# Node degrees by one-hot products: a count matrix of 64 rows by 98 columns in place of 128 by 49

## The chip, the cores and the metric

The kernel runs on one NeuronCore of a Trainium2 chip. The metric is the device time of one execution in microseconds (us). Three runs of the kernel before gave 1557.44 us as their median (1555.77 to 1563.06).

## The reference, cut to what matters

The program is one layer of a graph network over N = 6250 nodes with 256 features and E = 100,000 edges: layer norm, a graph convolution, a linear attention, and a mixture of experts. The change touches one term of the graph convolution, the number of edges that end in each node:

```python
deg = jax.ops.segment_sum(jnp.ones_like(dst_f, dtype=h.dtype), dst_f, num_segments=n)
dinv = jax.lax.rsqrt(deg)
norm = dinv[src_f] * dinv[dst_f]
out = jax.ops.segment_sum(h[src_f] * norm[:, None], dst_f, num_segments=n) + conv_bias
```

`dst_f` holds the 100,000 edge targets and one self loop per node, so deg is the count of edges into a node, plus one.

## The kernel before, in words

The kernel is a sequence of phases with a barrier of all engines between them. The change lies in the first one, which prepares the statistics, the degrees and the table of scaled node rows. Nodes lie as 49 tiles (T) of 128 partitions (P): node n is partition n mod 128 of tile n div 128.

**Preparation.** The edge targets are loaded as 98 rows of 512 (L239), turned by TensorE transposes of 98 by 128 blocks (L428), and copied out by ScalarE (L281) as 784 columns (NC) of 128 edges. VectorE splits each target into hi = target >> 7 and lo = target & 127 (L509, L510) and stores both as bf16 (L511, L512).

**Counting.** The 784 columns are taken in 56 blocks (OHB) of 14 (OHC). For each block VectorE writes two one-hot tiles by comparing with an iota: `ohlo`, 128 values by 14 columns (L533), and `ohhi`, 49 values by 14 columns (L534). TensorE then issues 14 products per block (L447), one per column c: stationary `ohlo[:, :, c]` (128 columns) and moving `ohhi[:, :, c]` (49 columns), both bf16, all summed into one PSUM tile of 128 by 49, which is the degree of node (partition, tile). The block's column is the last dimension of the one-hot tiles, so that neighbouring elements of both operands of a product lie 14 elements (28 bytes) apart. A ring of four pairs of tiles (OHR) joins the two engines: VectorE waits on `oh_free` (L530) before it overwrites a pair, TensorE on `oh_ok` (L445) before it reads one. Two products with an all-zero tile open and close the sum (L442, L450). There are 56 x 14 = 784 counting products.

**Beside it.** ScalarE computes sums (L290) and squared sums (L295) of the node rows. GpSimd (POOL) builds constants (L346 to L370), then waits for these sums and turns them into layer norm statistics (L375 to L395). VectorE's program has two reciprocals for them between its blocks: L541 stands after block 48, behind a wait for GpSimd, and L546 after block 52, behind a wait for ScalarE's square root (L310).

**After the count.** VectorE waits for the closing product, adds one (L553), ScalarE takes the square root (L312), VectorE forms the inverse root and the scale and bias of every node row (L556 to L563). Only then ScalarE scales the 49 tiles (L321), TensorE turns them (L456), VectorE and GpSimd copy them, and SP writes them to the table in memory (L265). The next phase gathers from that table.

A second stage later in the kernel has the same form and isn't touched: L1506 counts expert places by 14 products per round with a stationary of 128 columns and a moving operand of 105 columns, both bf16 and both 28 bytes apart from element to element.

Of the kernel before, what the change touches and what calls it, by code (L numbers as in the profile page):

```python
# [4 lines left out]
f32, i32, bf16, f16 = mybir.dt.float32, mybir.dt.int32, mybir.dt.bfloat16, mybir.dt.float16  # L5
i16 = mybir.dt.int16
ALU, ACT, AX = mybir.AluOpType, mybir.ActivationFunctionType, mybir.AxisListType
P = 128
# [6 lines left out]
T = -(-N // P)  # L15
# [8 lines left out]
OHC = 14  # L24
# [30 lines left out]
def build(nc, a_x, a_src, a_dst, a_gw, a_cb, a_lnw, a_lnb, a_pre, a_wqkv, a_mk, a_mv, a_wout, a_bout,  # L55
# [5 lines left out]
    with ExitStack() as ctx:  # L61
        def sb(name, shape, dt=f32):
            return ctx.enter_context(nc.sbuf_tensor(name, shape, dt))

        def semaphore(phase, name):

            phase.append(nc.alloc_semaphore(name))
            return phase[-1]
# [7 lines left out]
        R2 = sb("R2", [P, KC * NP])  # L76
# [36 lines left out]
        ident = sb("ident", [P, P])  # L113
# [18 lines left out]
        deg = sb("deg", [P, T])  # L132
# [20 lines left out]
        ps = [ctx.enter_context(nc.psum_tensor(f"ps{i}", [P, 512], f32)) for i in range(8)]  # L153
# [4 lines left out]
        class Chain:  # L158
# [5 lines left out]
            def done(self, ins):  # L164
# [12 lines left out]
        dTi = R3[:, 7000:7000 + NC].bitcast(i32)  # L177
        hiI = R3[:, 7800:7800 + NC].bitcast(i32)
        loI = R3[:, 8600:8600 + NC].bitcast(i32)
        hiB = R3[:, 9400:9400 + NC // 2].bitcast(bf16)  # L180
        loB = R3[:, 9800:9800 + NC // 2].bitcast(bf16)
        iox = RG[:, 0:P * OHC // 2].bitcast(bf16).rearrange("p (j c) -> p j c", c=OHC)
        ohlo = [R2[:, 1250 * k:1250 * k + P * OHC // 2].bitcast(bf16).rearrange("p (j c) -> p j c", c=OHC)
                for k in range(OHR)]
        ohhi = [R2[:, 1250 * k + 900:1250 * k + 900 + T * OHC // 2].bitcast(bf16).rearrange("p (j c) -> p j c", c=OHC)
                for k in range(OHR)]
        slowT = R3[:, 10200:10200 + NC].rearrange("p (g c) -> p g c", c=GC)
        zeroB = slotb[:, 0, 0:P // 2].bitcast(bf16)
        zslot = RG[:, 0:ZS * D].rearrange("p (s f) -> p s f", s=ZS)
        root3, val3, tmp3 = (RG[:, 3560 + 3 * T * k:3560 + 3 * T * (k + 1)] for k in range(3))  # L190
# [11 lines left out]
        phase = []  # L202
        with nc.Block() as block:
# [17 lines left out]
            oh_ok = semaphore(phase, "p_onehots_ready")  # L221
            oh_free = semaphore(phase, "p_onehots_free")
            deg_ok = semaphore(phase, "p_deg_ready")
            slow_ok = semaphore(phase, "p_outside_ready")
            slow_out = semaphore(phase, "p_outside_stored")
            root_in = semaphore(phase, "p_root_in")
# [110 lines left out]
            def _(pool):  # L337
                n = 0

                def step(ins):  # L340
# [7 lines left out]
                                             base=0, pattern=[[-1, P]], channel_multiplier=1))  # L348
# [9 lines left out]
                                             base=0, pattern=[[1, P]], channel_multiplier=-1))  # L358
                step(nc.gpsimd.affine_select(out=valid[:, :], in_=ones[:, 0:1], compare_op=ALU.is_gt, fill=0.0,
                                             base=TAIL, pattern=[[0, 1]], channel_multiplier=-1))  # L360
                step(nc.gpsimd.memset(inblk, 0.0))
                for a, b in DBLK:
                    step(nc.gpsimd.tensor_copy(inblk[:, a:b], ident[:, a:a + 1].to_broadcast([P, b - a])))
                step(nc.gpsimd.affine_select(out=isd[:, 0:1], in_=ones[:, 0:1], compare_op=ALU.is_gt, fill=0.0,
                                             base=ND, pattern=[[0, 1]], channel_multiplier=-1))
                step(nc.gpsimd.affine_select(out=isd[:, 1:2], in_=ones[:, 0:1], compare_op=ALU.is_ge, fill=float(WIN // DW),
                                             base=-ND, pattern=[[0, 1]], channel_multiplier=1))
# [2 lines left out]
                step(nc.gpsimd.tensor_copy(iokey[:, :], iokey_i))  # L370
                pool.sem_inc(const, 1)

                var, two = sc[:, :], slice(0, 2 * T)
                pool.wait_ge(sum_ok, 2 * T + 1)
                step(nc.gpsimd.tensor_scalar(var, ssq[:, :], 1.0 / D, None, ALU.mult))  # L375
# [38 lines left out]
            @block.tensor  # L414
            def _(pe):
                pe.sem_inc(oh_free, OHR)
                pe.sem_inc(zt_ok, 4)
                pe.wait_ge(const, 1)
                for n, arr in enumerate((dstf, relf, srcf)):
                    if n == 1:  # L420
                        pe.wait_ge(const, 3)
                        pe.wait_ge(least_ok, 1)
                        nc.tensor.matmul(ps[6][0:GH, 500:501], inblk[0:GH, 0:GH], least[0:GH, 0:1], start=True,
                                         stop=True).then_inc(first_ok, 1)
                    pe.wait_ge(rel_ok, n + 1)
                    for h in range(2):
                        for c in range(GC):
                            last = nc.tensor.transpose(ps[2 * n + h][:, c * GH:(c + 1) * GH],  # L428
                                                       arr[0:GH, h, c * P:(c + 1) * P], ident[0:GH, 0:GH])
                        last.then_inc(tr_ok, 1)  # L430

                pe.wait_ge(rel_ok, 4)
                for k in range(4):
                    nc.tensor.transpose(ps[6][0:1, k * GH:(k + 1) * GH], cols[0:GH, k:k + 1], ident[0:GH, 0:GH])
                pe.wait_ge(tr_ev, 1)
                for k in range(GC + 1):
                    last = nc.tensor.transpose(ps[0][0:1, k * GH:(k + 1) * GH], cols[0:GH, 4 + k:5 + k],
                                               ident[0:GH, 0:GH])
                last.then_inc(bt_ok, 1)

                pe.wait_ge(oh_ok, 1)
                nc.tensor.matmul(ps[7][:, 0:T], zeroB, zeroB[:, 0:T], start=True, stop=False)  # L442
                with nc.tensor.Fori(0, OHB // OHR) as i:
                    for k in range(OHR):
                        pe.wait_ge(oh_ok, i * OHR + (k + 2))  # L445
                        for c in range(OHC):
                            last = nc.tensor.matmul(ps[7][:, 0:T], ohlo[k][:, :, c], ohhi[k][:, :, c],  # L447
                                                    start=False, stop=False)
                        last.then_inc(oh_free, 1)
                nc.tensor.matmul(ps[7][:, 0:T], zeroB, zeroB[:, 0:T], start=False, stop=True).then_inc(deg_ok, 1)  # L450

                def flip(t, u):
                    pe.wait_ge(z_ok, t + 1)
                    pe.wait_ge(zt_ok, t + 1)
                    for k in range(KC):
                        last = nc.tensor.transpose(ps[u % 4][:, k * P:(k + 1) * P], zslot[:, u, k * P:(k + 1) * P],  # L456
                                                   ident[:, :])
                    last.then_inc(zt_ps, 1)

                with nc.tensor.Fori(0, T // ZS) as i:  # L460
                    for u in range(ZS):
                        flip(i * ZS + u, u)
                flip(T - 1, 0)

            @block.vector
            def _(v):
# [3 lines left out]
                ch = Chain(v, dv)  # L470
                v.wait_ge(d_in, 16 * 2)
                h = slice(0, GH)
# [18 lines left out]
                for c in range(GC):  # L491
                    last = nc.vector.tensor_scalar(relf[h, 0, c * P:(c + 1) * P], dstf[h, 0, c * P:(c + 1) * P],
                                                   cut[h, c:c + 1], None, ALU.subtract)
# [12 lines left out]
                v.wait_ge(tr_ev, 2)  # L506
                dflat = dT.rearrange("p g c -> p (g c)")
                ch.done(nc.vector.tensor_copy(dTi, dflat))
                ch.done(nc.vector.tensor_scalar(hiI, dTi, 7, None, ALU.arith_shift_right))  # L509
                ch.done(nc.vector.tensor_scalar(loI, dTi, P - 1, None, ALU.bitwise_and))  # L510
                ch.done(nc.vector.tensor_copy(hiB, hiI))  # L511
                ch.done(nc.vector.tensor_copy(loB, loI))  # L512

# [15 lines left out]
                def onehots(m, k):  # L529
                    v.wait_ge(oh_free, m + 1)  # L530
                    lo = loB[:, bass.ds(m * OHC, OHC)].unsqueeze(1)
                    hi = hiB[:, bass.ds(m * OHC, OHC)].unsqueeze(1)
                    nc.vector.tensor_tensor(ohlo[k], lo.to_broadcast([P, P, OHC]), iox, ALU.is_equal)  # L533
                    nc.vector.tensor_tensor(ohhi[k], hi.to_broadcast([P, T, OHC]), iox[:, 0:T, :],  # L534
                                            ALU.is_equal).then_inc(oh_ok, 1)

                with nc.vector.Fori(0, OHB // OHR - 2) as i:
                    for k in range(OHR):
                        onehots(i * OHR + k, k)
# [3 lines left out]
                for k in range(OHR):  # L543
                    onehots(OHB - 2 * OHR + k, k)
# [3 lines left out]
                for k in range(OHR):  # L548
                    onehots(OHB - OHR + k, k)

                v.wait_ge(deg_ok, 1)
                inv, fix = root3[:, 2 * T:3 * T], tmp3[:, 2 * T:3 * T]
                ch.done(nc.vector.tensor_scalar(deg[:, :], ps[7][:, 0:T], 1.0, None, ALU.add))  # L553
                v.sem_inc(root_in, 1)
                v.wait_ge(root_ok, 2)
                ch.done(nc.vector.reciprocal(inv, inv))  # L556
# [88 lines left out]
        phase = []  # L645
# [536 lines left out]
        phase = []  # L1182
# [146 lines left out]
        phase = []  # L1329
# [490 lines left out]
        phase = expert_phase  # L1820
# [222 lines left out]
```

## Time and profile before

| what | value |
|---|---|
| median of 3 runs | 1557.44 us (1555.77 to 1563.06) |
| the profiled execution | 1565.51 us |
| its span | 1563.7 us |
| TensorE matmuls (PE) busy | 1295.5 us, 83% |
| TensorE weight loads (PEld) busy | 1132.9 us, 72% |
| VectorE (DVE) busy | 987.5 us, 63% |
| GpSimd (POOL) busy | 870.6 us, 56% |
| ScalarE (ACT) busy | 525.8 us, 34% |

The busy shares are means over phases with different limits. For this change the first 145 us matter: the preparation up to about 26 us, the counting from about 26 to 111 us, and the scaled rows and the table from about 112 to 141 us. A matmul's duration in the rows is its latency, which overlaps with that of the next; how fast a series goes is read from the distance between starts.

### The profile page before, as it was taken

What the parts mean: (1) busy time and instruction counts of PE and PEld (TensorE: products, weight loads), DVE (VectorE), ACT (ScalarE), POOL (GpSimd) and SP (SyncE); (2) the same over time, 40 slices, a digit from 0 to 9 for tenths busy, and PEclk for the clock granted to TensorE, in tenths of its full rate; (3) what the DMA queues carried; (4) which work ended last, traced back from release to release, by engine and by line L of the source; (5) the groups of instructions that cost most, each with busy time, mean ns of one, the idle gap of its engine ahead of it and who ended that gap; (6) DMA issues with size and microseconds to landing.
All of it is one profiled execution on the core that took longest, in us unless ns stands there. A gap on an engine that the chain in (4) does not pass through costs nothing. (4 is left out here: it accounts for less than half of the span.)

```text
span 1563.7 us, 30532 instructions
## 1 busy us (share of the span) xinstructions
PE 1295.5 (83%) x8310; PEld 1132.9 (72%) x8311; DVE 987.5 (63%) x2911; ACT 525.8 (34%) x1415; POOL 870.6 (56%) x837
## 2 busy tenths in 40 slices
PE   4986587878867788879878879788569999999996
PEld 4974476767757677768767667566359999999996
DVE  7987466656556777667677548777844444444443
ACT  6608000111112222323331120133735555555553
POOL 2374666666666666666666631133027766676664
PEclk9998787999989999999998988899569999999998
DMA  7006332332345555556677760032944444444442
GB/s 216 0 0 208 88 88 86 88 89 85 88 125 146 151 166 169 172 170 190 193 237 225 244 199 1 14 108 95 331 53 71 68 69 70 66 74 69 72 66 35
DMA packets 138352, 183.07 MB, mean 117 GB/s; under 512 B 27256, under 2 KB 116036, under 8 KB 138124
## 3 DMA queue, kind: packets, MB, share of 16 engines
q0 software_dynamic: 44400, 92.92, 25.7%
q1 hardware_dynamic: 93852, 89.00, 19.0%
q8 instruction: 41, 0.67, 0.2%
q14 instruction: 59, 0.48, 0.1%
HBM read 149.38 MB, written 33.41 MB: 117 GB/s over the span
## 5 line engine op out<-in xcount | busy, mean ns | idle before, releaser
L729 POOL DMA_INDIRECT RG<-table,srci x504 | 492.1, 976 | 283.8 <-issue 126.9
L746 PEld LDWEIGHTS ps<-S_t,RG 128*128 128x128 f32 x2016 | 283.2, 208 | 32.7 <-issue 17.0
L746 PE MATMUL ps<-S_t,RG 128*128 128x96 f32 x2016 | 284.8, 288 | 16.7 <-issue 12.6
L1000 DVE TENSOR_TENSOR R<-R,ps 128x392 f32 x280 | 157.5, 562 | 184.2 <-PE ps L756 77.9
L768 PE MATMUL ps<-zrow,R 128*128 128x256 f32 x686 | 205.5, 404 | 30.9 <-DMA zrow<-table 16.4
L1990 POOL DMA_INDIRECT out<-R,S_t x105 | 166.7, 1588 | 98.3 <-DVE R L1960 55.0
L1873 PE MATMUL ps<-R,RG 128*128 128x128 f32 x1680 | 206.8, 277 | 0.0
L1883 PE MATMUL ps<-R 128*128 x840 | 198.5, 379 | 0.0
L1873 PEld LDWEIGHTS ps<-R,RG 128*128 128x128 f32 x1680 | 197.8, 193 | 0.3 <-issue 0.3
L1906 ACT ACTIVATE R<-ps,RG 128x128 f32<-128x128 f32 x420 | 120.1, 368 | 175.2 <-PE ps L1873 139.1
L1956 DVE TENSOR_TENSOR R<-ps,R 128x256 f32<-128x256 f32 x105 | 44.6, 425 | 200.6 <-PE ps L1883 198.8
L768 PEld LDWEIGHTS ps<-zrow,R 128*128 128x128 f32 x686 | 127.5, 200 | 56.6 <-DMA zrow<-table 27.2
L1883 PEld LDWEIGHTS ps<-R 128*128 128x128 f32 x840 | 151.7, 190 | 16.3
L1978 POOL DMA_INDIRECT R<-ntable,S_t x105 | 104.4, 994 | 90.1 <-PEq L1855 58.4
L872 ACT ACTIVATE R<-iwin 128x256 f32<-128x256 f32 (+2 forms) x127 | 60.3, 488 | 204.5 <-PE ps L768 131.8
L1915 ACT ACTIVATE RG<-R 128x1028 f32 x105 | 112.7, 1075 | 20.5 <-PEq L72 20.5
L1567 POOL TENSOR_TENSOR R<-R,slot 128x256 f32<-128x256 f32 x49 | 35.6, 728 | 111.1 <-DVE slot L1651 111.1
L447 PE MATMUL ps<-R 128*128 128x49 bf16 x784 | 80.7, 276 | 10.1 <-DVE R L534 10.0
L447 PEld LDWEIGHTS ps<-R 128*128 128x128 bf16 x784 | 72.8, 144 | 18.0 <-DVE R L534 11.9
L756 PE MATMUL ps<-ohk,ohs 128*128 128x392 bf16 x140 | 48.8, 350 | 33.4 <-issue 19.6
L1945 DVE TENSOR_SCALAR R<-ps,gamma,beta 128x128 f32<-128x128 f32 x212 | 76.2, 400 | 0.0
L959 DVE TENSOR_TENSOR S_t<-dstrel,iwin 128x384 f32<-128x384 f32 x126 | 69.4, 550 | 0.7
(362 smaller groups left out, 2026.3 us busy)
## 6 DMA issues: line engine op xcount, KB each, us to landing
zrow<-table SPq DMA_DIRECT2D x336, 128.0 KB
RG<-table,srci POOLq DMA_INDIRECT x504
table<-RG SPq DMA_DIRECT2D x12, 512.0 KB, 3.0
out<-R SPq DMA_DIRECT2D x12, 512.0 KB, 2.9
ntable<-R SPq DMA_DIRECT2D x12, 512.0 KB
R<-in_x SPq DMA_DIRECT2D x6, 896.0 KB
R<-in_w SPq DMA_DIRECT2D x8, 514.0 KB, 9.0
slot<-in_x SPq DMA_DIRECT2D x32, 128.0 KB
```

What stands on the lines that cost most here:

```text
L447: last = nc.tensor.matmul(ps[7][:, 0:T], ohlo[k][:, :, c], ohhi[k][:, :, c], start=False, stop=False)
L729: nc.gpsimd.indirect_dma_start(out=grows[:, s, :], out_offset=None, in_=table, in_offset=bass.IndirectOffsetOnAxis(ap=srci[:, ND + q, c:c ...
L746: last = nc.tensor.matmul(window(q % 2)[:, h, :], grows[:, s, h * P:(h + 1) * P], S_t[:, q % 2, c, :], start=c == 0, stop=c == GC - 1)
L768: nc.tensor.matmul(psD[:, 0:D], adj[b % 2][0:n, j, :], zrow[0:n, i % ZR, :], start=j == 0, stop=j == T - 1).then_inc(z_used, 1)
L1000: nc.vector.tensor_tensor(win, win, psK[m % 2][:, 0:T * DW].rearrange("p (j w) -> p j w", w=DW), ALU.add).then_inc(cnt_ok, 1)
L1873: last = nc.tensor.matmul(psH[s % 2][:, h * P:(h + 1) * P], w1r[:, s, k * HID + h * P:k * HID + (h + 1) * P], ur[:, s % 2, k, :], start=k ...
L1883: last = nc.tensor.matmul(psY[s % 2][:, 0:D], hr[:, s % 2, h, :], w2_sb[:, bass.ds(e, 1), h, :].rearrange("p a f -> p (a f)"), start=h == ...
L1906: last = act.activation(hr[:, s % 2, h, :], psH[s % 2][:, h * P:(h + 1) * P], ACT.Gelu, bias=w1r[:, s, KC * HID + h:KC * HID + h + 1])
L1915: act.activation(w1r[:, s, :], w1_sb[:, bass.ds(e, 1), :].rearrange("p a f -> p (a f)"), ACT.Copy).then_inc(c_ok, 1)
L1945: nc.vector.tensor_scalar(ur[:, s % 2, k, :], psX[s % 2][:, k * P:(k + 1) * P], gamma[:, k:k + 1], beta[:, k:k + 1], ALU.mult, ALU.add)
L1978: nc.gpsimd.indirect_dma_start(out=xr[:, t % 4, :], out_offset=None, in_=ntable, in_offset=bass.IndirectOffsetOnAxis(ap=gat[:, t:t + 1], a ...
L1990: nc.gpsimd.indirect_dma_start(out=a_out, out_offset=bass.IndirectOffsetOnAxis(ap=sct[:, t:t + 1], axis=0), in_=yr[:, t % 4, :], in_offset ...
```

## The change

The count matrix is 64 by 98: lo is now the low six bits of the target, hi the rest. The stationary one-hot tile has 64 columns, the moving one 98. At the end the two halves of a tile's 128 nodes lie in neighbouring columns of 64 rows. VectorE copies them apart into SBUF (`halfT`), and two fp32 products put them under each other in another PSUM bank: one with the upper 64 rows of the identity, one with a matrix `upper` that shifts by 64 rows, which GpSimd builds among its constants. The one-hot ring's tiles in SBUF are laid out anew for the new sizes. The number of blocks, their 14 columns, the ring of four, and the number of counting products stay.

```diff
+        cols2 = R2[:, 5100:5100 + 2 * T + P]
+        LO = P // 2
-        ohlo = [R2[:, 1250 * k:1250 * k + P * OHC // 2].bitcast(bf16).rearrange("p (j c) -> p j c", c=OHC)
+        ohlo = [R2[:, 1250 * k:1250 * k + LO * OHC // 2].bitcast(bf16).rearrange("p (j c) -> p j c", c=OHC)
                 for k in range(OHR)]
-        ohhi = [R2[:, 1250 * k + 900:1250 * k + 900 + T * OHC // 2].bitcast(bf16).rearrange("p (j c) -> p j c", c=OHC)
+        ohhi = [R2[:, 1250 * k + 500:1250 * k + 500 + T * OHC].bitcast(bf16).rearrange("p (j c) -> p j c", c=OHC)
                 for k in range(OHR)]
+        halfT, upper = cols2[:, 0:2 * T], cols2[:, 2 * T:2 * T + P]
...
+                step(nc.gpsimd.memset(upper, 0.0))
+                step(nc.gpsimd.affine_select(out=upper, in_=upper, compare_op=ALU.not_equal, fill=1.0, base=LO,
+                                             pattern=[[-1, P]], channel_multiplier=1))
+                pool.sem_inc(half_ok, 1)
...
-                            last = nc.tensor.matmul(ps[7][:, 0:T], ohlo[k][:, :, c], ohhi[k][:, :, c],
+                            last = nc.tensor.matmul(ps[7][0:LO, 0:2 * T], ohlo[k][:, :, c], ohhi[k][:, :, c],
                                                     start=False, stop=False)
...
-                nc.tensor.matmul(ps[7][:, 0:T], zeroB, zeroB[:, 0:T], start=False, stop=True).then_inc(deg_ok, 1)
+                nc.tensor.matmul(ps[7][0:LO, 0:2 * T], zeroB[:, 0:LO], zeroB[:, 0:2 * T], start=False,
+                                 stop=True).then_inc(deg_ok, 1)
+                pe.wait_ge(half_ok, 2)
+                nc.tensor.matmul(ps[6][:, 0:T], ident[0:LO, :], halfT[0:LO, 0:T], start=True, stop=False)
+                nc.tensor.matmul(ps[6][:, 0:T], upper[0:LO, :], halfT[0:LO, T:2 * T], start=False,
+                                 stop=True).then_inc(deg_ok, 1)
...
-                ch.done(nc.vector.tensor_scalar(hiI, dTi, 7, None, ALU.arith_shift_right))
-                ch.done(nc.vector.tensor_scalar(loI, dTi, P - 1, None, ALU.bitwise_and))
+                ch.done(nc.vector.tensor_scalar(hiI, dTi, 6, None, ALU.arith_shift_right))
+                ch.done(nc.vector.tensor_scalar(loI, dTi, LO - 1, None, ALU.bitwise_and))
...
-                    nc.vector.tensor_tensor(ohlo[k], lo.to_broadcast([P, P, OHC]), iox, ALU.is_equal)
-                    nc.vector.tensor_tensor(ohhi[k], hi.to_broadcast([P, T, OHC]), iox[:, 0:T, :],
+                    nc.vector.tensor_tensor(ohlo[k], lo.to_broadcast([P, LO, OHC]), iox[:, 0:LO, :], ALU.is_equal)
+                    nc.vector.tensor_tensor(ohhi[k], hi.to_broadcast([P, 2 * T, OHC]), iox[:, 0:2 * T, :],
                                             ALU.is_equal).then_inc(oh_ok, 1)
...
                 v.wait_ge(deg_ok, 1)
+                ch.done(nc.vector.tensor_copy(halfT[0:LO, :].rearrange("p (h t) -> p h t", h=2),
+                                              ps[7][0:LO, 0:2 * T].rearrange("p (t h) -> p h t", h=2)))
+                v.sem_inc(half_ok, 1)
+                v.wait_ge(deg_ok, 2)
-                ch.done(nc.vector.tensor_scalar(deg[:, :], ps[7][:, 0:T], 1.0, None, ALU.add))
+                ch.done(nc.vector.tensor_scalar(deg[:, :], ps[6][:, 0:T], 1.0, None, ALU.add))
```

## Rows read from the trace of the kernel before

**Rows 1.** Groups by line, 0 to 260 us: count, busy us, mean ns, idle before.

```profile
L447 PE MATMUL ps<-R 128*128 128x49 bf16 x784 | 80.7, 276 | 10.1 <-DVE R L534 10.0
L533 DVE TENSOR_TENSOR R<-R,RG 128x1792 bf16<-128x1792 bf16 x56 | 61.7, 1101 | 0.7 <-DVE flag_i L526 0.3 <-DVE RG L546 0.2 <-DVE RG L541 0.2
```

**Rows 2.** Timeline, first blocks and steady state: start us, us, what.

```profile
26.23 1.09 DVE L533 TENSOR_TENSOR R<-R,RG 128x1792 bf16<-128x1792 bf16 x1 [0.34 <-DVE flag_i L526]
27.24 0.51 DVE L534 TENSOR_TENSOR R<-R,RG 128x686 bf16<-128x686 bf16 x1
27.80 1.31 PEld L447 LDWEIGHTS ps<-R 128*128 128x128 bf16 x14 [7.13 <-DVE R L534]
...
43.38 1.08 DVE L533 TENSOR_TENSOR R<-R,RG 128x1792 bf16<-128x1792 bf16 x1
44.38 0.51 DVE L534 TENSOR_TENSOR R<-R,RG 128x686 bf16<-128x686 bf16 x1
44.81 1.08 DVE L533 TENSOR_TENSOR R<-R,RG 128x1792 bf16<-128x1792 bf16 x1
```

**Rows 3.** Timeline, one late block by itself, and the end of the count.

```profile
101.13 1.51 PE L447 MATMUL ps<-R 128*128 128x49 bf16 x14 [0.22 <-DVE R L534]
...
111.51 0.22 PE L450 MATMUL ps<-slotb 128*128 128x49 bf16 x1
111.77 0.21 DVE L553 TENSOR_SCALAR deg<-ps 128x49 f32<-128x49 f32 x1 [1.65 <-PE ps L450]
...
114.36 6.01 ACT L321 ACTIVATE RG<-R,zs_b,zs_s 128x256 f32<-128x256 f32 x12 [2.04 <-DVEq L564]
```

**Rows 4.** Timeline of the second counting stage, its first two rounds.

```profile
1121.89 5.61 PE L1506 MATMUL ps<-R 128*128 128x105 bf16 x28 [7.55 <-DVE R L1772]
```

**Rows 5.** Lines L1506 and L1502: duration ns min/median/max, first and last start.

```profile
L1506 PE MATMUL ps<-R x98: 368/373/391, 1121.9 to 1142.4; 128*128 128x105 bf16 x98
...
L1502 PE MATMUL ps<-slotb x1: 271/271/271, 1114.1 to 1114.1; 128*128 128x105 bf16 x1
```

**Rows 6.** Two stretches: length, PE busy us, granted clock, DMA share, GB/s.

```profile
28.00:95.00 67.00, 67.00 (x659) 1.00 0.01 2
...
1122.00:1142.00 20.00, 18.90 (x96) 0.50 1.22 261
```

**Rows 7.** Timeline: fp32 transposes, and weight loads in pairs.

```profile
7.07 1.54 PE L428 MATMUL ps<-ident,R 98*128 98x98 f32 x8 [7.07 <-DVEq L475]
...
120.42 0.29 PEld L456 LDWEIGHTS ps<-ident,RG 128*128 128x128 f32 x2 [0.20 <-ACT RG L321]
120.91 0.20 PEld L456 LDWEIGHTS ps<-ident,RG 128*128 128x128 f32 x2 [0.20 <-ACT RG L321]
```

**Rows 8.** Timeline of L1492: loads of 49 columns for products of one column.

```profile
1108.33 1.57 PEld L1492 LDWEIGHTS ps<-ones,R 128*49 128x49 f32 x16 [10.08 <-DVEq L1717]
```

**Rows 9.** Timeline: an fp32 product, its reader, and a PSUM read of 98 columns.

```profile
11.34 0.49 PE L423 MATMUL ps<-least,S_t 98*98 98x1 f32 x2 [2.73 <-POOLq L368]
...
11.94 0.16 DVE L482 COPY cols<-ps 98x1 f32<-98x1 f32 x1 [2.35 <-PE ps L423]
...
25.08 0.25 DVE L524 CAST first_i<-ps 1x98 int32<-1x98 f32 x1
```

**Rows 10.** Timeline of GpSimd's constants and statistics, and of what they release.

```profile
0.79 0.20 POOL L346 MEMSET ident<- 128x128 f32 x1 [0.29 <-POOLq L2033]
1.24 0.29 POOL L347 TENSOR_SCALAR_AFFINE_SELECT ident<-ident 128x128 f32<-128x128 f32 x1 [0.25 <-POOL ident L346]
...
63.28 31.82 POOL L375 TENSOR_SCALAR sc<-ssq 128x49 f32<-128x49 f32 x1 [50.84 <-ACT slot L295]
...
95.62 0.47 DVE L541 RECIPROCAL RG<-RG 128x49 f32<-128x49 f32 x1 [0.74 <-POOLq L377]
...
97.81 0.29 ACT L310 ACTIVATE RG<-RG 128x98 f32<-128x98 f32 x1 [33.32 <-POOLq L381]
...
109.95 0.38 POOL L395 TENSOR_SCALAR cq<-cq 128x49 f32<-128x49 f32 x1
```

More of the change, by code:

```diff
@@ L223, in build @@
             deg_ok = semaphore(phase, "p_deg_ready")
+            half_ok = semaphore(phase, "p_half_rows")
             slow_ok = semaphore(phase, "p_outside_ready")
@@ L441, in _ @@
                 pe.wait_ge(oh_ok, 1)
-                nc.tensor.matmul(ps[7][:, 0:T], zeroB, zeroB[:, 0:T], start=True, stop=False)
+                nc.tensor.matmul(ps[7][0:LO, 0:2 * T], zeroB[:, 0:LO], zeroB[:, 0:2 * T], start=True, stop=False)
                 with nc.tensor.Fori(0, OHB // OHR) as i:
```

## The prediction

> **What bounds the kernel now.** I read the groups by line for the stage first: 784 counting products and 56 pairs of one-hot writes, and nearly all idle time that TensorE has before a counting product (10.0 of 10.1 us) ends with VectorE's second one-hot write, L534 [rows 1]. Then the timeline, to see who sets the pace. VectorE starts L533 at 43.38, L534 at 44.38 and the next L533 at 44.81: 1.00 us for 1792 elements and 0.43 us for 686, so 1.43 us a block and no gap [rows 2]. TensorE's own pace shows where a block stands alone: 14 products in 1.51 us of which the last 0.276 us are its latency, so 13 distances in 1.234 us, 95 ns each [rows 1, 3], 1.33 us a block. VectorE bounds the count, by 1.43 to 1.33: TensorE has 7% to spare. The count is wholly on the path. After its closing product at 111.51 come L553 on VectorE at 111.77, and the scaled rows on ScalarE only from 114.36 [rows 3]; a barrier ends the phase, so what the count gains or loses moves the rest of the kernel.
>
> **The change on VectorE.** From the two sizes, (1.00 - 0.43) us / (1792 - 686) = 0.515 ns an element and about 0.08 us fixed [rows 2]. The new tiles have 64 x 14 = 896 and 98 x 14 = 1372 elements: 0.54 and 0.78 us, 1.32 us a block. That is 0.11 us less, 6.2 us over 56 blocks, if VectorE stayed the bound.
>
> **The change on TensorE.** The products stay 784, and each moves 98 columns in place of 49. What a moving column costs in this layout, 28 bytes from one to the next, is the number on which all hangs, and there are two rows for it. At 49 columns the distance is 95 ns [rows 1, 3]. The second counting stage has the same stationary tile of 128 columns, the same 28 bytes, and 105 moving columns: 28 products in 5.61 us, less the last one's 0.373 us, is 27 distances of 194 ns [rows 4, 5]. So 56 columns more cost 99 ns, 1.77 ns each, and 98 columns give 95 + 49 x 1.77 = 182 ns. A plain ratio, 194 x 98 / 105, gives 181. That the distance between columns in memory is the cause shows in the latency: with the closely packed zero tile a product of 105 columns took 271 ns, the spaced ones 373 [rows 5]; at 49 columns it is 0.22 us against 276 ns [rows 1, 3].
>
> Both rows must stand for the same clock to be set on one line. The second stage has 0.50, the lower level of 1.2 GHz. The profile shows 1.00 for the first [rows 6], but I don't believe it: L428's eight transposes of 98 columns, of which the last has 0.37 us of latency, start 0.167 us apart, and the loads of L456 fall from 0.29 to 0.20 us a pair only between 120.42 and 120.91 [rows 7]. The packed products agree: 0.22 us at 49 columns [rows 3] and 271 ns at 105 [rows 5] differ by 0.86 to 0.9 ns a column, one cycle of 1.2 GHz. So the count ran at the lower level from start to end, and the rise came behind it.
>
> Here the Trainium skill speaks on both sides. "SBUF — State Buffer" says of reads that each access which leaves a 16-byte line pays a penalty; at 28 bytes each moving column does, and the trace agrees (373 against 271 ns). "TensorE: Matmul & The Clock Gate", section "Back-to-back issue gap", gives N/1.2 ns at the lower clock, 82 ns for 98 columns, with which TensorE would stay under VectorE; by the same rule 105 columns take 88 ns, where the trace has 194, so the rows decide.
>
> TensorE then needs 14 x 182 = 2.55 us a block against VectorE's 1.32: the bound changes sides. Rows for the price run from 1.67 ns a column (0.167 us for L428's 98 fp32 columns [rows 7]: 164 ns) to 1.94 (95 ns for 49 [rows 3]: 190 ns). I take 182, which lies between two rows of this very form.
>
> **Weight loads.** 64 stationary columns in place of 128. No row has this load in bf16. The nearest narrow one is L1492: 16 loads of 49 columns in 1.57 us, about 93 ns each with its product of one column [rows 8]; scaled to 64 columns 122 ns. From below it is nothing. In the second stage loads of 128 columns lie beside products of 194 ns without making them longer than the line above, so I put 122 under 182 at nothing. If that cover failed, it would be a rival, below.
>
> **Sum for the count.** The first pair of tiles is ready at 26.23 + 0.54 + 0.86 (the second's full duration, 0.78 + 0.08) = 27.63, the first load 0.05 us later, as 27.80 follows 27.24 + 0.51 now [rows 2]: 27.68. From there TensorE runs without a gap, since the ring of four fills: 784 x 0.182 = 142.7, hence the closing product at 170.3 in place of 111.51: +58.8. At the 181.5 between both estimates, which I use, it is +58.5. VectorE now waits on oh_free (L530) over a microsecond in each block.
>
> **What stands behind that wait.** The reciprocal L541 follows block 48, which VectorE can write once block 44 is consumed: 27.7 + 44 x 2.54 = 139 us. GpSimd's L375 took 31.82 us, until VectorE paused, and L541 came at 95.62, so GpSimd seems kept out by VectorE's writes [rows 10]; pauses in each block let it in sooner. From L541 to ScalarE's root at 97.81 is 2.2 us, from there to the last statistics at 109.95 is 12 us, and TensorE has four blocks (10 us) and then four more in hand. Both hide, also with 2 us more. Without that cover each would cost its 2.2 us.
>
> **Tail.** Added on the path between L450 and L553: the copy of 98 columns from PSUM, 0.25 us, and two fp32 products. One product, from its start to its reader, is 11.94 - 11.34 = 0.60 us, and a second adds up to its 0.49 [rows 9]. With two hand-overs of about 0.05 us: 1.4 us. Ends: 0.9 and 2.0.
>
> **The rest.** GpSimd's memset and select, 0.20 and 0.29 us, with their own waits under 1 us [rows 10], lie at about 12.4 us; GpSimd idles 50.84 us until 63.28 [rows 10], and `half_ok` is wanted only at 170. Shift and mask keep their sizes. No DMA is added.
>
> Sum: +58.5 + 1.4 = **+59.9 us**. The profiled execution's 1565.5 would become 1625.4; it stands 8.1 us over the median. On the median: 1557.4 + 59.9 = **1617.3 us**.
>
> **Rivals.**
> 1. *The loads don't hide.* A narrow load that can't go in beside the running product adds its 122 ns: 784 x 0.304 = 238 us, +154.5 in place of +58.5, 1713 us. For it: no row has such a load beside a long product, and the Trainium skill ("TensorE: Matmul & The Clock Gate", section "Weight-path perf modes") keeps its fast load for 128 columns. Against: at 128 columns loads and products overlap [rows 4].
> 2. *The clock rises in the count, and TensorE keeps up (not slower).* If it goes to 2.4 GHz in the middle of the work and the spaced reads halve with it, the distance is 91 ns, 1.27 us a block, under VectorE's 1.32. Then VectorE saves 6.2 us, the tail costs 1.4: 1552.6 us. It decides from 94 ns (1.32 us / 14) down. For it: the fp32 loads did fall with the clock [rows 7]. Against: the second stage, busy 18.90 of 20.00 us with products of nearly this form, stayed at 0.50 [rows 6].
> 3. *Spacing costs latency, not pace.* Then what holds the products apart is something else that doesn't grow with the columns, and 98 of them stay near 95 ns, 1.33 us a block: level with VectorE's 1.32, some 1553 us. It decides from the same 94 ns. Against it are the 194 ns at 105 columns [rows 4]. This is the mechanism that the Trainium skill's gap above would imply.
>
> **How the numbers follow.** Forecast 0.89, rival 1 0.05, rival 2 0.04, rival 3 0.02. Ends of the forecast: 784 x 0.164 = 128.6, +44.4 + 0.9 gives 1603; 784 x 0.190 = 149.0, +65.1 + 2.0 gives 1625, and 3 us for the scatter of the runs above their median gives 1628. I give 1604 to 1628. A measurement here tells about 0.5% (7.8 us) from no change. The forecast and rival 1 are slower; rivals 2 and 3, at -4.8 us, lie within 0.5%, with a little beyond it: faster 0.01, same 0.05, slower 0.94.
>
> **What would show it.** Right: matmul starts in L447 180 ns apart with none waiting on L534; VectorE's pair in 1.32 us followed by over 1 us idle before L533, released by TensorE; L450 near 170 us; two fp32 products and 1.4 us more before L553; later phases shifted and otherwise the same. Wrong: distances of 300 ns with loads that start only after a product (rival 1), loads and products shortened in the middle of the count (rival 2), or VectorE still without gaps (rivals 2, 3).

## The result, and the profile after

The changed kernel takes 1620.69 us (median of 4 runs, 1610.84 to 1626.39), the kernel before 1556.61 us (median of 4) beside it. It is slower by 64 us on the medians, a ratio of 1.041; the estimate over all runs is a ratio of 1.0378 with a 95% interval of 1.0335 to 1.0422, which is 59 us. The prediction had said 1617, 60 us more. The profiled execution took 1626.30 us with a span of 1624.5.

The profile after, first the groups by line of the first 330 us. The counting products are now line L456, VectorE's writes L547 and L548; the rows answer to [rows 1].

```profile
L456 PE MATMUL ps<-R 128*64 128x98 bf16 x784 | 141.0, 359 | 6.6 <-DVE R L548 6.6
L548 DVE TENSOR_TENSOR R<-R,RG 128x1372 bf16<-128x1372 bf16 x56 | 48.8, 872 | 0.0
L547 DVE TENSOR_TENSOR R<-R,RG 128x896 bf16<-128x896 bf16 x56 | 35.0, 626 | 54.3 <-PE ps L456 54.0 <-DVE flag_i L540 0.3
```

The idle time has changed sides. TensorE waits for VectorE once, for the first block; VectorE waits 54.0 us for TensorE. The timeline of the first blocks (start us, us, what), against [rows 2], and of the end, against [rows 3] (TensorE's row L456 is from the view of 27 to 60 us):

```profile
26.24 0.63 DVE L547 TENSOR_TENSOR R<-R,RG 128x896 bf16<-128x896 bf16 x1 [0.34 <-DVE flag_i L540]
26.78 0.87 DVE L548 TENSOR_TENSOR R<-R,RG 128x1372 bf16<-128x1372 bf16 x1
27.56 0.62 DVE L547 TENSOR_TENSOR R<-R,RG 128x896 bf16<-128x896 bf16 x1
27.70 32.56 PE L456 MATMUL ps<-R 128*64 128x98 bf16 x180 [6.58 <-DVE R L548]
...
168.52 0.26 PE L459 MATMUL ps<-slotb 128*64 128x98 bf16 x1
168.82 0.25 DVE L566 COPY R<-ps 64x98 f32<-64x98 f32 x1 [8.72 <-PE ps L459]
169.18 0.66 PE L462 MATMUL ps<-R,ident 64*128 64x49 f32 x2 [0.40 <-DVEq L568]
169.64 0.62 PE L463 MATMUL ps<-R 64*128 64x49 f32 x2
170.30 0.21 DVE L571 TENSOR_SCALAR deg<-ps 128x49 f32<-128x49 f32 x1 [1.23 <-PE ps L463]
...
172.89 5.53 ACT L325 ACTIVATE RG<-R,zs_b,zs_s 128x256 f32<-128x256 f32 x11 [2.04 <-DVEq L582]
```

180 products in 32.56 us, less the last one's 0.36, are 179 distances of 180 ns; before it was 95. VectorE needs 27.56 - 26.24 = 1.32 us for a block. The closing product comes at 168.52 in place of 111.51 (+57.0), L571 1.78 us later where L553 came 0.26 us later (+1.5), and the scaled rows at 172.89 in place of 114.36: +58.5 us, the lot of it from the count and its tail. The spans differ by 60.8; the 2.3 us between lie in the later phases and are less than the scatter of the runs.

### The profile page after: what moved, and what is told of

It is laid out like the page before. It is cut to its first block and busy times, and to the rows that moved or that the text cites. A ratio compares the mean times of both kernels' runs of the same rounds, so it can differ in the third digit from the quotient of the medians.

```text
span 1624.5 us, 30546 instructions
## 1 busy us (share of the span) xinstructions
PE 1372.0 (84%) x8314; PEld 1215.2 (75%) x8315; DVE 989.6 (61%) x2912; ACT 526.2 (32%) x1415; POOL 838.4 (52%) x839
## 5 line engine op out<-in xcount | busy, mean ns | idle before, releaser
L764 PEld LDWEIGHTS ps<-S_t,RG 128*128 128x128 f32 x2016 | 291.7, 213 | 30.1 <-issue 12.3
L764 PE MATMUL ps<-S_t,RG 128*128 128x96 f32 x2016 | 291.6, 293 | 12.9 <-issue 7.7
L456 PE MATMUL ps<-R 128*64 128x98 bf16 x784 | 141.0, 359 | 6.6 <-DVE R L548 6.6
L456 PEld LDWEIGHTS ps<-R 128*64 128x64 bf16 x784 | 140.7, 195 | 6.7 <-DVE R L548 6.7
```

Source lines behind the costliest of these rows:

```text
L456: last = nc.tensor.matmul(ps[7][0:LO, 0:2 * T], ohlo[k][:, :, c], ohhi[k][:, :, c], start=False, stop=False)
L764: last = nc.tensor.matmul(window(q % 2)[:, h, :], grows[:, s, h * P:(h + 1) * P], S_t[:, q % 2, c, :], start=c == 0, stop=c == GC - 1)
```

## The experiments

Twelve experiments were run, in four groups, each on another chip and with its own runs of the kernel before: 1560.67 us (one run) beside experiments 1 to 4, 1432.81 (23 runs) beside 5 to 8, 1563.19 (17 runs) beside 9 to 11, 1571.44 (one run) beside 12. Times are compared only within a group. Kernels of which the text names no number of runs had one run each; the four runs of the changed kernel spread over 15 us, so such a time says little by itself, and the readings rest on the timelines. The products' distances and the ends of the count don't have this spread.

**Theory A**: what costs is the step in memory from one moving column to the next, in time per column. **Theory B**: it is the narrow load of 64 columns. Four kernels, all made from the kernel after, change one operand each.

**1. Moving columns packed**

```diff
-  last = nc.tensor.matmul(ps[7][0:LO, 0:2 * T], ohlo[k][:, :, c], ohhi[k][:, :, c],
+  last = nc.tensor.matmul(ps[7][0:LO, 0:2 * T], ohlo[k][:, :, c],
+                          ohhi[k].rearrange("p j c -> p (j c)")[:, c * 2 * T:(c + 1) * 2 * T],
```

> The kernel after, but each product reads its 98 moving columns packed (2 bytes apart) from the same tile, so the degrees are not those of the reference; sizes, counts and VectorE's work stay. Theory A (the spacing of the moving columns sets TensorE's pace, 1.77 ns a column): distances in L456 fall from 180 ns to what the 64 spaced stationary columns need, between 94 and 122 ns; the closing product comes between 101 us (VectorE-bound, 1.32 us a block) and 123 us instead of 168.5, the whole near 1552 to 1575 us. Theory B (the narrow 64-column load is what costs): distances stay at 180 ns, near 1620 us.

**2. Stationary columns packed**

```diff
-  last = nc.tensor.matmul(ps[7][0:LO, 0:2 * T], ohlo[k][:, :, c], ohhi[k][:, :, c],
+  last = nc.tensor.matmul(ps[7][0:LO, 0:2 * T], ohlo[k].rearrange("p j c -> p (j c)")[:, c * LO:(c + 1) * LO],
+                          ohhi[k][:, :, c],
```

> The kernel after, but each product reads its 64 stationary columns packed, so the degrees are not those of the reference. Theory A: distances stay at 180 ns and the closing product at 168 us, the whole 1611 to 1626 us as after. Theory B: distances fall below 130 ns and the whole below 1585 us.

**3. Half the moving columns**

```diff
-  last = nc.tensor.matmul(ps[7][0:LO, 0:2 * T], ohlo[k][:, :, c], ohhi[k][:, :, c],
+  last = nc.tensor.matmul(ps[7][0:LO, 0:T], ohlo[k][:, :, c], ohhi[k][:, 0:T, c],
```

> The kernel after, but each product moves only 49 of the 98 columns (targets of the upper half are not counted); stationary stays 64 columns, VectorE's work stays. Theory A: distances of 95 ns as before the change, 1.33 us a block, level with VectorE's 1.32; closing product near 102 us, the whole near 1554 us. Theory B: the 64-column load shows, distances between 122 and 180 ns, closing product at 123 us or later, the whole 1575 us or more.

**4. Stationary tile of 128 columns again** (the tiles are laid out further apart for it, and the zero products widened)

```diff
-  last = nc.tensor.matmul(ps[7][0:LO, 0:2 * T], ohlo[k][:, :, c], ohhi[k][:, :, c],
+  last = nc.tensor.matmul(ps[7][:, 0:2 * T], ohlo[k][:, :, c], ohhi[k][:, :, c],
...
-  nc.vector.tensor_tensor(ohlo[k], lo.to_broadcast([P, LO, OHC]), iox[:, 0:LO, :], ALU.is_equal)
+  nc.vector.tensor_tensor(ohlo[k], lo.to_broadcast([P, P, OHC]), iox, ALU.is_equal)
```

> The kernel after with a stationary one-hot of 128 columns again (the upper 64 rows of the count stay zero), 98 moving columns; VectorE's block grows from 1.32 to 1.78 us. Theory A: distances 180 to 182 ns, closing product near 168 us, the whole 1611 to 1626 us. Theory B: with the wide load distances go to about 100 ns, VectorE bounds with 1.78 us a block, closing product near 127 us, the whole near 1579 us.

Measured: 1582.25, 1620.98, 1575.96 and 1628.68 us, the kernel before 1560.67. The same stretch of the timeline, 27.5 to 60 us, TensorE's products, one fence for each kernel in the order above:

```profile
27.70 32.59 PE L456 MATMUL ps<-R 128*64 128x98 bf16 x277 [6.58 <-DVE R L549]
```
```profile
27.69 32.65 PE L456 MATMUL ps<-R 128*64 128x98 bf16 x183 [6.59 <-DVE R L549]
```
```profile
27.70 32.48 PE L456 MATMUL ps<-R 128*64 128x49 bf16 x272 [6.58 <-DVE R L548]
```
```profile
28.16 32.17 PE L456 MATMUL ps<-R 128*128 128x98 bf16 x176 [7.20 <-DVE R L548]
```

The same time holds 277, 183, 272 and 176 products. With their latencies (0.32, 0.36, 0.30 and 0.36 us) taken off, the distances are 117, 177, 119 and 182 ns. Packing the stationary tile takes 3 ns away (177) and widening it nothing (182), so B falls as the cause of the 180 ns. Packing the moving columns (117) or halving them (119) takes about the same 62 ns away and then stops. That floor is the same for 98 packed and for 49 spaced columns, and what both share is the load of 64 spaced columns. That it is the load's step, and not the 64 rows or the narrow tile, is seen in experiment 7, where 64 paired by 98 paired columns go at 81 ns.

The third expectation failed in this: A alone had said 95 ns and 1554 us, and 119 ns and 1575.96 us came out. Two whole times missed their ranges as well, 1582.25 against 1552 to 1575 in the first and 1628.68 against 1611 to 1626 in the fourth, though their distances (117 and 182 ns) came as theory A had them. Both theories name a real bound, and the larger one counts. The closing product came at 119.30 in the first and at 120.71 in the third kernel, against 111.51 before the change: had moving columns been free, the change would still have lost 8 us in the count through its narrow load.

**5 and 6. What each operand costs before the change**

Two kernels made from the kernel before, one operand packed in each.

```diff
-  last = nc.tensor.matmul(ps[7][:, 0:T], ohlo[k][:, :, c], ohhi[k][:, :, c],
+  last = nc.tensor.matmul(ps[7][:, 0:T], ohlo[k][:, :, c],
+                          ohhi[k].rearrange("p j c -> p (j c)")[:, c * T:(c + 1) * T],
```

> The kernel before with its 49 moving columns read packed, so the degrees are not those of the reference. If the 95 ns between products were the price of 49 spaced moving columns, they fall inside a block, to between 41 and 80 ns; if the fast load of 128 spaced columns set them, they stay at 95 ns. The whole stays at 1557 us (VectorE bounds).

```diff
-  last = nc.tensor.matmul(ps[7][:, 0:T], ohlo[k][:, :, c], ohhi[k][:, :, c],
+  last = nc.tensor.matmul(ps[7][:, 0:T], ohlo[k].rearrange("p j c -> p (j c)")[:, c * P:(c + 1) * P],
+                          ohhi[k][:, :, c],
```

> The kernel before with its 128 stationary columns read packed, so the degrees are not those of the reference. If the moving columns set the 95 ns, they stay (93 to 95); if the load set them, they fall. The whole stays at 1557 us.

Measured: 1430.60 and 1431.43 us, before 1432.81 in that group: VectorE bounds, as expected (the 1557 us of the expectations belong to the first group). One block in each timeline, moving packed first:

```profile
101.07 1.04 PE L447 MATMUL ps<-R 128*128 128x49 bf16 x14 [0.69 <-DVE R L535]
```
```profile
101.08 1.44 PE L447 MATMUL ps<-R 128*128 128x49 bf16 x14 [0.30 <-DVE R L535]
```

Less latencies of 0.24 and 0.27 us: 62 and 90 ns. The second lies a little under the 93 to 95 ns that were expected. So the 95 ns before the change were, but for the 5 ns that packing the load takes away, the price of 49 spaced moving columns, as the prediction's line through 95 and 194 ns assumed. The load of 128 spaced columns costs no more than 62 ns, and that of 64 costs 117: half the columns, nearly twice the time. The Trainium skill ("TensorE: Matmul & The Clock Gate", section "Weight-path perf modes") keeps its fast load for full loads of 128 columns that aren't fp32, and the trace agrees.

**7 and 8. The one-hot tiles in pairs**

The tiles keep their sizes, but block columns lie in pairs: [7][values][2] in place of [values][14], so that both operands have 4 bytes from column to column. The same edit was made to the kernel after (64 by 98) and to that before (128 by 49).

```diff
-  iox = RG[:, 0:P * OHC // 2].bitcast(bf16).rearrange("p (j c) -> p j c", c=OHC)
+  iox = RG[:, 0:P].bitcast(bf16).rearrange("p (j c) -> p j c", c=2)
...
-  ohlo = ....rearrange("p (j c) -> p j c", c=OHC)
+  ohlo = ....rearrange("p (o j c) -> p o j c", o=OHC // 2, c=2)
...
-  ... iota(iox[:, :, :], pattern=[[1, P], [0, OHC]] ...
+  ... iota(iox[:, :, :], pattern=[[1, P], [0, 2]] ...
...
-  last = nc.tensor.matmul(..., ohlo[k][:, :, c], ohhi[k][:, :, c],
+  last = nc.tensor.matmul(..., ohlo[k][:, c // 2, :, c % 2], ohhi[k][:, c // 2, :, c % 2],
...
-  nc.vector.tensor_tensor(ohlo[k], lo.to_broadcast([P, LO, OHC]), iox[:, 0:LO, :], ALU.is_equal)
+  nc.vector.tensor_tensor(ohlo[k], lo.to_broadcast([P, OHC // 2, LO, 2]),
+                          iox[:, 0:LO, :].unsqueeze(1).to_broadcast([P, OHC // 2, LO, 2]), ALU.is_equal)
```

> The change kept (64 by 98), but the one-hot tiles laid out in pairs of block columns, so that both operands of a product have 4 bytes from column to column in place of 28; the result is the reference's. Theory A (crossing to far addresses at each column is the price): both bounds on TensorE fall, distances at or under 94 ns, VectorE bounds with 1.32 us a block, closing product near 102 us, the whole 1552 us, 5 us under the kernel before. Rival 1 (a narrow load costs 118 ns in any layout): closing product at 120 us, about 1572 us. Rival 2 (VectorE loses its rate on runs of two elements, twice the time): 2.5 us a block, closing product near 166 us, about 1617 us.

> The kernel before (128 by 49) with the same pair layout. Theory A: TensorE's distances fall below 95 ns, VectorE still bounds with 1.43 us a block, so the time is that of before, 1557 us within 0.5%. If VectorE loses its rate on runs of two: 2.7 us a block, about 1630 us.

Measured, 12 runs each against 23 of before in the same group (1432.81 us): 64 by 98 took 1424.71 us, a ratio of 0.9947 (0.9929 to 0.9965); 128 by 49 took 1428.40 us, 0.9975 (0.9958 to 0.9991). The groups by line of the 64 by 98 kernel (20 to 180 us), then two of its blocks, one by its loads and one by its products:

```profile
L456 PE MATMUL ps<-R 128*64 128x98 bf16 x784 | 54.3, 229 | 29.8 <-DVE R L549 29.5
L549 DVE TENSOR_TENSOR R<-R,RG 128x1372 bf16<-128x1372 bf16 x56 | 48.8, 872 | 0.0
L547 DVE TENSOR_TENSOR R<-R,RG 128x896 bf16<-128x896 bf16 x56 | 35.0, 626 | 0.7 <-DVE flag_i L540 0.3 <-DVE RG L562 0.2 <-DVE RG L557 0.2
```
```profile
25.98 1.16 PEld L456 LDWEIGHTS ps<-R 128*64 128x64 bf16 x14 [0.15 <-DVE R L549]
...
31.25 0.84 PE L456 MATMUL ps<-R 128*64 128x98 bf16 x14 [0.41 <-DVE R L549]
```

VectorE pays nothing for runs of two (872 and 626 ns as in the changed kernel), TensorE now waits for it in each block, and the idle time is back on TensorE's side. Both pair rivals fall. Rival 1 in particular: a narrow load does not cost 118 ns in any layout, for the first of the two rows is a block at TensorE's lower clock whose loads, and with them the products, start 81 ns apart. The second is at its upper one (13 distances in 0.84 less 0.20 us, 49 ns); the clock rose at about 30 us in this kernel alone of experiments 1 to 8. The gain does not hang on that, since 14 x 81 ns = 1.13 us is under VectorE's 1.32 too.

From the first counting load to the closing product it is 24.66 to 102.00, 77.3 us, in the 64 by 98 kernel and 24.75 to 107.66, 82.9 us, in the other: the 5.6 us that the smaller comparison was worth once TensorE keeps up, where the prediction's working had 6.2. But both start 3 us earlier than the kernel before (27.80), which no expectation had; that the closing product came at 102.00, just where it was expected, is partly luck for that reason. What gave the 3 us was asked next.

**9. The iota later**

```diff
-  step(nc.gpsimd.iota(iox[:, :, :], pattern=[[1, P], [0, OHC]], ...))     (after ident)
...
+  step(nc.gpsimd.iota(iox[:, :, :], pattern=[[1, P], [0, OHC]], ...))     (after isd, before iokey)
+  pool.sem_inc(const, 1)
...
-  v.wait_ge(const, 2)
+  v.wait_ge(const, 4)
```

> The kernel before with GpSimd's iota of 1792 elements (4.6 us) moved behind the constants that TensorE's L423 waits for. Theory: the pair layout's short iota gave 3 us of the gain of the runs with it, because L423 waited for GpSimd. Then this kernel alone starts the count 3 us earlier (first counting load at 24.8 instead of 27.8) and ends 3 us (0.2%) under before. Rival: the iota isn't on the path, no change.

Measured: 1563.82 us (12 runs) against 1563.19, a ratio of 0.9997 (0.9972 to 1.0022): no change, and the count starts at 27.43, 0.4 us earlier and not 3. The expectation failed, but not in the wait that it named. The timeline of this kernel (TensorE's L424 is L423 of the kernel before):

```profile
4.67 0.69 DVE L475 CAST R<-R 98x1024 f32<-98x1024 int32 x1
...
6.76 0.69 DVE L478 TENSOR_REDUCE least<-R 98x4 f32<-98x512 f32 x1
7.60 3.71 DVE L481 TENSOR_SCALAR R<-R,cols 98x512 f32<-98x512 f32 x1 [0.15 <-DVE least L478]
...
7.66 0.46 PE L424 MATMUL ps<-least,S_t 98*98 98x1 f32 x2 [0.55 <-DVEq L480]
...
11.35 0.16 DVE L483 COPY cols<-ps 98x1 f32<-98x1 f32 x1
```
```profile
6.42 4.61 POOL L367 IOTA RG<- 128x1792 bf16 x1 [0.17 <-POOL isd L364]
```

and the same two VectorE steps in the kernel before, where GpSimd's iota runs from 1.70 to 6.31:

```profile
4.53 2.34 DVE L474 CAST R<-R 98x1024 f32<-98x1024 int32 x1
...
9.10 0.48 DVE L480 TENSOR_SCALAR R<-R,cols 98x512 f32<-98x512 f32 x1
```

In the kernel before, VectorE is done with the subtraction at 9.58 and stands until 11.94, because L423 waits for GpSimd's constants until 11.34 [rows 9]. This wait was as the theory had it, and moving the iota removed it: L424 starts at 7.66. What the theory lacked is that the iota holds VectorE as well. It stretches the VectorE cast or subtraction that it meets to about its own end: the cast from 0.69 to 2.34 us, the subtraction from 0.48 to 3.71, and the copy behind it comes at 11.35 in place of 11.94. The reduction between them takes its 0.69 us beside the iota as without it. The pair kernels' iota is short (1.54 us), their cast takes 0.70 us, and L423 starts at 8.29 in place of 11.34 [rows 9]: they are free of both. So the 3 us belong to the short iota, the only part of the pair layout that acts before the count, though it was not run by itself. Of the pair kernel's gain of 8 us about 5 are the count's, the longer tail taken off.

**10. The change once more**

> The changed kernel once more, beside the two others on one chip, since the kernel before took 1433 us on the second chip and 1557 us on the first. Theory: the change costs the same microseconds in the count (closing product at 168.5, +57 and 1.5 us of tail) on either, so +59 us within the scatter of 5 us, whatever the later phases take.

Measured: 1624.97 us (6 runs) against 1563.19, a ratio of 1.0403 (1.0367 to 1.0439), 62 us. Closing product at 168.51, L571 at 170.30, as in the first profile. The 3 us that this is over the forecast 59 lie within the 5 us of scatter that it allowed. The kernel before took about the same here as beside the result, so this says nothing of a chip where it takes 1433 us; there the changed kernel was not run.

**11 and 12. Dense work beside the count, for the clock**

Open was rival 2: what spaced reads cost at 2.4 GHz. Dense products of 512 packed columns were put ahead of each block of the kernel after, four with zeros as their stationary tile at first, then sixteen with one-hot values there.

```diff
+  pe.wait_ge(tr_ev, 6)
...
   pe.wait_ge(oh_ok, i * OHR + (k + 2))
+  for _ in range(4):
+      nc.tensor.matmul(ps[5][:, 0:512], zeroB, iox.rearrange("p j c -> p (j c)")[:, 0:512], start=True, stop=True)
```

> The kernel after with four dense products of 512 packed columns (zero weights, into a PSUM bank that nothing else uses then) ahead of each block's 14, to bring TensorE's clock to its upper level during the count; the result is the reference's. It asks what the spaced reads cost at 2.4 GHz. If the clock stays at 1.2 GHz: dense products 427 ns, spaced ones 180 ns, 4.2 us a block. If it rises and the spaced reads follow it (rival 2 of the prediction): 216 and about 91 ns, 2.1 us a block. If it rises and they don't follow (their price is in the memory): 216 and about 180 ns, 3.4 us a block.

> As the run with four dense products, which left TensorE at its lower level, but with 16 of them ahead of each block, and one-hot values in place of zeros as their stationary tile; the result is the reference's. If the clock now rises and the spaced reads follow it: dense 216 ns, spaced about 91 ns. If it rises and they don't: dense 216 ns, spaced 160 to 180 ns. If the clock stays low: 427 and 180 ns, 9.4 us a block, and rival 2 stays open.

With four the clock stayed: the dense products are 427 ns apart, the spaced ones 180, in 1739.67 us.

```profile
43.04 2.76 PE L460 MATMUL ps<-R 128*64 128x98 bf16 x14
45.73 1.89 PE L457 MATMUL ps<-RG,slotb 128*128 128x512 bf16 x4
```

With sixteen (1871.03 us) it rose; number and values were changed together, so which of them raised it is not shown. Its timeline of TensorE from 200 us on:

```profile
200.38 5.31 PE L457 MATMUL ps<-RG,R 128*128 128x512 bf16 x16
205.62 2.76 PE L460 MATMUL ps<-R 128*64 128x98 bf16 x14
208.31 3.63 PE L457 MATMUL ps<-RG,R 128*128 128x512 bf16 x15
211.87 2.75 PE L460 MATMUL ps<-R 128*64 128x98 bf16 x14
```

The dense products show the level: the series at 208.31 is 216 ns from start to start, 512 columns at 2.4 GHz, and that at 200.38 is a mix of both levels. The granted clock of the stretches says the same: 0.59 from 200.38 to 203.00, 1.00 from 205.62 to 211.87. The 14 spaced products behind either series take 2.75 to 2.76 us, with the 2.76 of the kernel with four at the lower level beside them; behind the first one, which stands apart, they start 179 to 180 ns apart in both. A spaced column costs the same at both levels. Its price is in nanoseconds and not in TensorE's cycles, so a rise of the clock alone, the condition of rival 2, can't help the change.

## Why the prediction was right, point by point

- **The bound changes sides**: right. L547 waits 54.0 us over 51 blocks, 1.06 us each, forecast as over a microsecond.
- **Distance between products**: 181.5 ns forecast, 180 measured. The line through two rows of the same form, 49 and 105 columns, was sound because both were bound by moving columns; experiments 5 and 6 (62 and 90 ns) show that for 49. The measured prices are 95, 180, 182 and 194 ns for 49, 98, 98 and 105 spaced columns.
- **Start and end of the count**: first load 27.68 forecast, 27.70 measured; closing product 170.0 at 181.5 ns, 168.52 measured. The count's term was +58.5 and came to +57.0.
- **VectorE's block**: 1.32 us forecast and measured.
- **The clock**: the reading that the count ran at 1.2 GHz although the column showed 1.00 is borne out by experiment 11, where the column shows 1.00 from 43 to 47 us as well and the dense products are 427 ns apart. That both rows stood for the same clock, on which the prediction insisted, was not needed: at 2.4 GHz the spaced products keep their 180 ns. (The packed products' difference is (271 - 220) / 56 = 0.91 ns a column and not "0.86 to 0.9"; nothing rests on it.)
- **Loads**: put at nothing behind the moving columns, with 122 ns as the other end. They hide (182 ns with the wide load, 180 with the narrow), and the narrow load's own price is 117. That the 122 came so near is partly luck: it was scaled from fp32 loads of another size. Rival 1, their sum, did not come.
- **What stands behind the wait**: L541's successor came at 140.03 (139 forecast), and the last statistics step started at 155.43, 13 us ahead of the closing product. GpSimd was let in sooner, as argued: its step at 63.23 takes 0.39 us in place of 31.82 [rows 10], shown below. It saves nothing, since nobody waited.
- **Tail**: +1.4 forecast, +1.5 measured (the copy 0.25 us, the products from 169.18 to the reader at 170.30).
- **Sum**: +59.9 forecast; +58.5 up to the scaled rows, +60.8 in the spans, +64 on the medians. That the profiled execution, at 1626.30 us, lies within 1 us of the 1625.4 forecast for it is luck, with runs that spread over 15 us. The range's lower end had a slip: 0.167 us for 98 columns is 1.70 ns each and not 1.67, which puts that end 2 us higher, still far below the result. Rival 3, spacing without a price in pace, is refuted by experiment 1.

```profile
63.23 0.39 POOL L384 TENSOR_SCALAR sc<-ssq 128x49 f32<-128x49 f32 x1 [49.97 <-ACT slot L299]
```

What the prediction lacked is that two bounds rose, not one. It weighed the narrow load only as an addend on top of 182 ns. Taken by itself, 14 x 117 = 1.64 us already lies over VectorE's old 1.43, so the change was lost on either operand. Rival 3's price was out of reach for the same reason: 98 columns at 95 ns stand under a load of 117.

## What to carry to other kernels

When a product's operands are slices with a wide step, cost each operand by itself and take the larger, each from a row with its own size and step (the load's price does not go with its columns: 117 ns for 64, at most 62 for 128); a balance of tile sizes that looks good on VectorE's element count (162 for 177 here) can double the product. Find the price of a moving column from two series of the same form in the trace and not from one. If the layout can be cut so that neighbouring columns lie 4 bytes apart, here at no cost to VectorE, the same change turns from 4% slower to 0.5% faster (measured on another chip), about 5 of its 8 us from the count and 3 from the shorter iota.

## What the runs showed of the hardware that was not expected

- A moving column 28 bytes from the last costs 1.84 ns at TensorE's lower level and at its upper one alike (180 ns for 98), a packed or paired one about 0.84 ns at the lower level (41 ns for 49 paired columns) and 0.42 to 0.5 at the upper (216 ns for 512 packed ones, 49 for 98 paired).
- A load of 64 bf16 columns with that step costs 117 ns, one of 128 columns at most 62 (both at the lower level); with 4 bytes from column to column the load of 64 costs at most 81 ns there.
- GpSimd and VectorE hold each other up: an iota of 4.61 us on GpSimd stretched a VectorE cast from 0.69 to 2.34 us and a subtraction from 0.48 to 3.71, but left a reduction at its 0.69. VectorE's gapless comparisons held a GpSimd step for 31.82 us that takes 0.39 with pauses; it took 26.61 to 31.83 us in the kernels whose VectorE had no pauses then, 0.39 to 0.84 where it had them. The Trainium skill ("SBUF — State Buffer", section "Who interferes with whom") says that casts and tensor_scalar steps of VectorE can contend with GpSimd, that a VectorE step with two SBUF inputs contends with a GpSimd step that reads SBUF, and that tensor_reduce never contends on this chip; the trace agrees in all three, with the numbers above.
- The same kernel before took 1433 us on one chip and 1557 to 1571 us elsewhere. In the kernel of experiment 6, from the first of these, the count is as ever (27.78 to 111.37 us, with 27.80 to 111.51 in the profile before), and GpSimd's gathers (L729 of before) sat idle 158.5 us in place of 283.8. The other profiles of that chip show 158.5 too, those of the others 280 to 292. Why was not tried; it is the reason why times are compared within a group only.
